# A twelve-stage decoder on one core: the l1 attention in two phases, the l3 convolution as matrix products, and a lower planned cost for products with narrow weights

## The reference, cut to what matters

```python
# l1 attention, 16 heads of 8 features (W block-diagonal per head)
Q, K, V = xh @ Wq, xh @ Wk, xh @ Wv          # xh: layer norm of x, by head
scores  = where(causal, Q @ K.T / sqrt(8), -1e9)
out     = softmax(scores) @ V                # 512 x 512 scores per head
y       = scrambled(out) @ W_O
# l3 attention, a selective scan over 256 channels with 16 states
x, gate = split(layernorm(h) @ in_proj_w + in_proj_b)
x = silu(depthwise_causal_conv(x, conv_w, K=4) + conv_b)
dt_r, Bm, Cm = split(x @ x_proj_w); dt = softplus(dt_r @ dt_proj_w + dt_proj_b)
h_t = exp(dt*A) * h_{t-1} + dt * B_t * x_t;  y_t = h_t . C_t     # 512 steps
out = (sigmoid(gate) * (y + x*D)) @ out_proj_w + out_proj_b + h
```

## Time and profile before

| | |
|---|---|
| median of 3 runs | 2419.95 us (2417.05 to 2420.04) |
| profiled execution, its own time | 2421.95 us |
| its span, first to last instruction | 2420.2 us (1.75 us lie around it) |
| busy: PE, DVE, ACT, POOL | 1886.7, 1694.5, 1019.4, 595.4 us |
| mean granted TensorE clock | 0.833 of full |
| l1 attention, both lanes | about 702 to 1009 us |
| l3 attention, both lanes | about 1711 to 2188 us |

### The profile page before, as it was taken

One profiled execution on the slowest core, in us unless ns is written; L12 is line 12 of the kernel. 1 busy time (PEld: TensorE's weight loads), 2 busy tenths in 40 slices (PEclk: granted clock), 3 DMA queues, 4 the chain that ended last, 5 costly groups with the idle time before them and its releaser, 6 DMA issues. The chain is left out here.

```text
span 2420.2 us, 30708 instructions
## 1 busy us (share of the span) xinstructions
PE 1886.7 (78%) x11122; PEld 1067.2 (44%) x11122; DVE 1694.5 (70%) x3758; ACT 1019.4 (42%) x1610; POOL 595.4 (25%) x528
## 2 busy tenths in 40 slices
PE   4878888889786676799998777669866666689983
PEld 2544645555452222466676655545531222234331
DVE  6666757575767767643637988994479989976556
ACT  1227556565644353443333233232245345335562
POOL 0003323242430010000001643530135534631100
PEclk8888998989996686899999877866668977879975
DMA  4002112120310000000000000000000000000000
GB/s 163 1 0 59 44 47 54 35 67 24 78 62 30 1 1 1 14 10 1 1 1 1 1 1 1 1 1 1 1 0 1 1 0 0 1 1 1 1 5 14
DMA packets 19222, 43.78 MB, mean 18 GB/s; under 512 B 5323, under 2 KB 7935, under 8 KB 18175
## 3 DMA queue, kind: packets, MB, share of 16 engines
q1 hardware_dynamic: 19071, 41.81, 6.1%
HBM read 16.63 MB, written 1.05 MB: 7 GB/s over the span
## 5 line engine op out<-in xcount | busy, mean ns | idle before, releaser
L2275 PE MATMUL lane_banks<-l_attn_lane_hc,base 128*128 128x512 f32 x256 | 168.9, 784 | 91.8 <-DVE l_attn_lane_hc L2430 91.5
L2357 POOL TENSOR_TENSOR l_attn_lane_u<-l_attn_lane_xp,l_attn_lane_bn 128x512 f32<-128x512 f32 x128 | 177.7, 1410 | 208.5 <-ACT l_attn_lane_bn L2328 166.4
L2421 DVE TENSOR_TENSOR_SCAN l_attn_lane_h<-l_attn_lane_da,l_attn_lane_u 128x512 f32<-128x512 f32 x128 | 194.5, 1542 | 6.6 <-ACT l_attn_lane_da L2336 5.5
L595 POOL TENSOR_SCALAR lane_next_rstd<-lane_next_mv 128x4 f32<-128x4 f32 x48 | 12.8, 267 | 717.0 <-DVE lane_next_mv L572 717.0
L1654 ACT ACTIVATE l_ffn_lane_hT<-lane_banks,weights 128x512 f32<-128x512 f32 x128 | 87.9, 687 | 146.2 <-PE lane_banks L1608 145.7
L1451 ACT ACTIVATE l_attn_lane_ex<-lane_banks 128x256 f32<-128x256 f32 (+3 forms) x128 | 82.9, 705 | 149.9 <-PE lane_banks L1409 149.9
L1700 DVE SCALAR_TENSOR_TENSOR l_ffn_lane_eo<-lane_banks,l_ffn_lane_sel,l_ffn_lane_eo 128x128 f32<-128x128 f32 x224 | 63.0, 343 | 96.6 <-PE lane_banks L1630 96.2
L1630 PEld LDWEIGHTS lane_banks<-weights,l_ffn_lane_hT 128*128 128x128 f32 x1024 | 121.2, 194 | 18.6 <-issue 15.2
L2275 PEld LDWEIGHTS lane_banks<-l_attn_lane_hc,base 128*128 128x128 f32 x256 | 52.4, 229 | 170.6 <-DVE l_attn_lane_hc L2430 143.8
L1630 PE MATMUL lane_banks<-weights,l_ffn_lane_hT 128*128 128x128 f32 x1024 | 124.0, 278 | 4.1 <-DVE l_ffn_lane_eo L1700 3.2
L2328 ACT ACTIVATE l_attn_lane_bn<-lane_banks 128x512 f32<-128x512 f32 x64 | 37.9, 594 | 179.1 <-PE lane_banks L2269 179.1
(11 more groups left out here) (526 smaller groups left out, 4693.6 us busy)
## 6 DMA issues: line engine op xcount, KB each, us to landing
f_attn_lane_vb<-f_attn_lane_work SPq DMA_DIRECT2D x192, 64.0 KB, 2.0
weights<-packed SPq DMA_DIRECT2D x1, 4564.5 KB, 13.6
f_attn_lane_work<-f_attn_lane_work SPq DMA_DIRECT2D x64, 64.0 KB, 2.0
f_attn_lane_vb<-f_attn_lane_va SPq DMA_DIRECT2D x8, 512.0 KB, 4.5
f_attn_lane_vb<-f_attn_lane_va SPq DMA_DIRECT2D x8, 384.0 KB, 5.8
weights<-packed SPq DMA_DIRECT2D x1, 2320.0 KB, 8.1
weights<-packed SPq DMA_DIRECT2D x1, 2091.0 KB, 13.9
out<-x SPq DMA_DIRECT2D x4, 256.0 KB, 2.2
```

The lines of the kernel that those rows point to most:

```text
L2275: pe.matmul(ps(2 + c), w("ident"), hc[:, c, :], start=(n == 1), stop=(n == NS)).then_inc(*s.up("state_added"))
L2357: g.tensor_tensor(u[:, i % 3, :], dtx[:, c, :], bn[:, n % 2, :], ALU.mult).then_inc(*s.up("u_ready"))
L2421: v.tensor_tensor_scan(h[:, c, :], da[:, i % 3, :], u[:, i % 3, :], 0.0, ALU.mult, ALU.add).then_inc(*s.up("scanned"))
```

## The change

In the l1 attention the row maxima of all four sets are taken first: the scores come in pairs of banks, two banks being filled while VectorE reduces the other two (32 reductions of two banks in a row of the batch instead of 16 of four). All maxima are negated at once (`mp` has four sets now), turned set by set into the four banks, and added. Then all exps follow: a set has ten steps of one full bank of 512 columns (key tile 0 of one head; tiles 1 and 3 of one head; tile 2 of two heads), which take banks 0 to 2 in turn; `heads` takes a turn too. `ex` has eight slots of 512 columns. `apply` comes three times a set and is placed some steps later, in the next set for the last two. `oS` is double and lies in `rest`. In the l3 attention the taps become eight f32 products with diagonal weights per row of the batch, accumulated in banks 3 and 0; bias and sigmoid read PSUM. `z` has a buffer of its own. The weights of this stage grow from 1510 to 2526 columns. The planner's cost of a product whose weights have at most 32 columns is multiplied by 0.3.

```diff
+def diagonals(w):
+    out = np.zeros((P, A3_C, A3_K, P), w.dtype)
+    for c in range(A3_C):
+        for k in range(A3_K):
+            out[np.arange(P), c, k, np.arange(P)] = w[c * P:(c + 1) * P, k]
+    return out.reshape(P, -1)
...
 def l1_attn(net, ln, row, s, sb, enter):
...
-    mp = sb("mp", [P, NT, R, 32], BF16)
-    ex = sb("ex", [P, 2, R, T])
-    oS = sb("oS", [P, T])
+    mp = sb("mp", [P, SETS, NT, R, 32], BF16)
+    STEPS, SLOTS = 10, 8
+    ex = sb("ex", [P, SLOTS, T])
+    oS = rest
...
+    users = []
+    for j in range(SETS):
+        users += [(j, i) for i in range(4)] + ([("heads", j - 1)] if j else []) + [(j, i) for i in range(4, STEPS)]
+    users.append(("heads", SETS - 1))
+    def turn(user):
+        return ps(users.index(user) % 3)
+    def wait_turn(pe, user):
+        n = users.index(user) - 3
+        if n < 0:
+            pe.wait_ge(*s.at("maxima_ready", n + 4))
+        else:
+            j, i = users[n]
+            if j == "heads":
+                pe.wait_ge(*s.at("cat_ready", i + 1))
+            else:
+                pe.wait_ge(*s.at("exp_done", STEPS * j + i + 1))
...
+        def apply(j, k):
+            yield
+            pe.wait_ge(*s.at("later_only", 8 * j + (2, 6, 8)[k]))
+            if k == 0:
+                if j >= 1:
+                    pe.wait_ge(*s.at("oS_ready", j))
+                else:
+                    pe.wait_ge(*s.at("maxima_ready", SETS))
+                for r in range(R):
+                    last = product(j, r, 0, ex[:, slot(j, r), :])
+            elif k == 1:
+                for r in range(R):
+                    product(j, r, 1, ex[:, slot(j, 4 + r), 0:3 * P])
+                for r in range(R):
+                    last = product(j, r, 3, ex[:, slot(j, 4 + r), 3 * P:T])
...
+        def keyed(j, i):
+            yield
+            wait_turn(pe, (j, i))
...
+            for r, kt in [(i, 0)] if i < 4 else [(i - 4, 1), (i - 4, 3)] if i < 8 else [(i - 8, 2), (i - 6, 2)]:
+                e, p, n = r % 2, 2 * j + r // 2, T - P * kt
+                last = pe.matmul(turn((j, i))[:, at:at + n], ops[half[e], p, 1, tile(kt)], ops[half[e], p, 0, P * kt:T], start=True, stop=True)
+                at += n
+            last.then_inc(*s.up("keyed_in_psum"))
...
+        for n in range(2 * NT * SETS):
+            j, g, b = n // (2 * NT), n // 2 % NT, n % 2
+            t, to = ORDER[g], P * (ORDER[g] + 1)
+            yield
+            if n >= 2:
+                pe.wait_ge(*s.at("row_max", n - 1))
+            for bank in (2 * b, 2 * b + 1):
+                r = late.index(bank)
+                early, p = group[bank ^ 1], 2 * j + r // 2
+                pe.matmul(ps(bank, 0, to), ops[early, p, 0, tile(t)], ops[early, p, 1, 0:to], start=True, stop=False)
+            for bank in (2 * b, 2 * b + 1):
+                last = pe.matmul(ps(bank, to - P, to), net.w16("ident16"), net.w16("later16"), start=False, stop=True)
+            last.then_inc(*s.up("scores_in_psum"))
...
+        for j in range(SETS):
+            for i in range(STEPS):
+                if j >= 1 and i == 0:
+                    yield from apply(j - 1, 1)
+                if j >= 1 and i == 2:
+                    yield from apply(j - 1, 2)
+                if j >= 1 and i == 4:
+                    yield from heads(j - 1)
+                if i == 6:
+                    yield from apply(j, 0)
+                yield from keyed(j, i)
...
+                act.activation(ex[:, slot(j, i), :], turn((j, i)), ACT.Exp, scale=scale).then_inc(*s.up("exp_done"))
...
+            v.tensor_reduce(mx[:, j, t, 2 * b:2 * b + 2], banks(2 * b, 2)[:, :, 0:to], AX.X, ALU.max).then_inc(*s.up("row_max"))
...
 def l3_attn(net, ln, row, s, sb, enter):
...
+        for c in range(C):
+            yield
+            pe.wait_ge(*s.at("xp_ready", c + 1))
+            pe.wait_ge(*s.at("sigmoids_ready", c + 1))
+            for j in range(A3_K):
+                k = A3_K * c + j
+                last = pe.matmul(ps(conv_bank[c]), w("a3_cw", k * P, (k + 1) * P), xp[:, c, j:j + T], start=(j == 0), stop=(j == A3_K - 1))
+            last.then_inc(*s.up("conv_in_psum"))
...
-            act.wait_ge(*s.at("conv_ready", c + 1))
-            act.activation(sgc[:, c, :], cv[:, c, :], ACT.Sigmoid).then_inc(*s.up("conv_sigmoid"))
+            act.wait_ge(*s.at("conv_in_psum", c + 1))
+            act.activation(sgc[:, c, :], ps(conv_bank[c]), ACT.Sigmoid, bias=w("a3_cb", c, c + 1)).then_inc(*s.up("conv_sigmoid"))
...
-        for j in range(A3_K):
-            for c in range(C):
-                k = A3_K * c
-                yield
-                if j == 0:
...
-                    v.tensor_scalar(cv[:, c, :], xp[:, c, 0:T], w("a3_cw", k, k + 1), w("a3_cb", c, c + 1), ALU.mult, ALU.add)\
...
-                    v.scalar_tensor_tensor(out=cv[:, c, :], in0=xp[:, c, j:j + T], scalar=w("a3_cw", k + j, k + j + 1),
-                                           in1=cv[:, c, :], op0=ALU.mult, op1=ALU.add)\
...
-            v.tensor_tensor(xs[:, c, :], cv[:, c, :], sgc[:, c, :], ALU.mult).then_inc(*s.up("xs_ready"))
+            v.scalar_tensor_tensor(out=xs[:, c, :], in0=ps(conv_bank[c]), scalar=w("a3_cb", c, c + 1), in1=sgc[:, c, :],
+                                   op0=ALU.add, op1=ALU.mult).then_inc(*s.up("xs_ready"))
...
     def matmul(self, out, lhsT, rhs, start, stop):
         rows = lhsT.shape[0]
         share = 0.3 if rows <= 32 else 0.6 if rows <= 64 else 1.0
+        share *= 0.3 if lhsT.shape[-1] <= 32 else 1.0
```

More of the change, by code:

```diff
@@ L1402, in tensor @@
-            for g in range(PAIRS):
-                kt, p = g // 2, 2 * j + g % 2
-                n = T - P * kt
-                yield
-                if g >= 1:
-                    pe.wait_ge(*s.at("exp_done", PAIRS * j + g))
-                for e in range(2):
-                    last = pe.matmul(ps(e, 0, n), ops[half[e], p, 1, tile(kt)], ops[half[e], p, 0, P * kt:T], start=True, stop=True)
-                last.then_inc(*s.up("keyed_in_psum"))
-                if g % 2 == 0 and kt >= 1:
-                    yield from apply(j, kt - 1)
@@ L1413, in tensor @@
-            yield from apply(j, NT - 1)
+        for j in range(SETS):
[9 more added lines that the diff above has]
+                yield from keyed(j, i)
+        yield from apply(SETS - 1, 1)
@@ L1414, in tensor @@
+        yield from apply(SETS - 1, 2)
+        yield from norm.tensor(pe, ps(2), norm.to_come)
         yield from heads(SETS - 1)
-        yield from norm.tensor(pe, ps(1), norm.to_come)
         yield
@@ L1465, in gpsimd @@
         g.wait_ge(*s.at("va_zeroed", 2))
-        g.memset(mp[:, :, :, :], 0.0).then_inc(*s.up("va_filled"))
+        g.memset(mp[:, :, :, :, :], 0.0).then_inc(*s.up("va_filled"))
         for i, name in enumerate("qk"):
@@ L1493, in finish @@
             v.wait_ge(*s.at("heads_in_psum", j + 1))
-            heads = ps(2).rearrange("p (t r f) -> p t r f", t=NT, r=R)
+            heads = turn(("heads", j)).rearrange("p (t r f) -> p t r f", t=NT, r=R)
             st.link(v.reciprocal(rden[:, j, :, :], heads[:, :, :, A1_HD]))
@@ L1523, in vector @@
             pair = ops[:, 2 * j:2 * j + 2, 0, :]
-            v.tensor_tensor(pair, pair, bc(ps(0).bitcast(BF16)[:, 0:T], 2), ALU.add).then_inc(*s.up("maxima_ready"))
-            for g in range(PAIRS):
-                kt, h = g // 2, 2 * (g % 2)
-                yield
-                v.wait_ge(*s.at("exp_done", PAIRS * j + g + 1))
-                first = ex[:, kt % 2, h:h + 2, 0:P]
-                v.tensor_tensor(first, first, bc(w("laterT"), 2), ALU.min).then_inc(*s.up("later_only"))
+            v.tensor_tensor(pair, pair, bc(maxima(j), 2), ALU.add).then_inc(*s.up("maxima_ready"))
+        for j in range(SETS):
+            if j == 2:
+                yield from norm.vector(v)
+            for i in (1, 3, 4, 5, 6, 7, 8, 9):
+                if j >= 1 and i == 4:
+                    yield from finish(j - 1)
+                yield from keep_later(j, i)
         yield from finish(SETS - 1)
```

122 lines of the change are left out of this document (53 added, 69 removed).

## The result

The changed kernel takes **2351.6 us**, median of 4 runs (2348.2 to 2353.0), beside 2420.0 for the kernel before on the same chip: ratio 0.9717 [0.9700, 0.9733]. The profiled execution took 2353.02 us (span 2351.2), 68.9 less than the one of before; the forecast was 43.

A forecast was written before the change was run, and what follows sets the result against it. No engine bounds the whole; l1 attention alternates one-engine phases with changeovers, and VectorE bounds l3 attention. -34 and -9 sum to -43 from 2421.95, giving 2379, or a 2377 us median; range 2338 to 2412.

The forecast's parts named there:

- Maxima and exps: l1 attention: per pair of sets 12.3 maxima, 1.4 additions, 12.6 exps; with one changeover 107.7 against 124.7 us a pass.
- rival 1: l1 attention: lanes cover each other, VectorE alone bounds at 92 us a pass; -64 for both, kernel 2347; chance 0.18.
- The extra reduction: l1 maxima: each of eight added reductions costs 0.07 to 0.15 us, 0.9 us for eight; TensorE's filling stays hidden.
- The unpaired products: l1 exps: keyed products in one partition half lose overlap; 2.0 us charged, making TensorE 12.2 us a pair.
- rival 2: l1 exps: TensorE bounds, keyed products never overlap, clock stays near 0.73; no l1 gain, kernel 2411; chance 0.16.
- The clock in the exps: l1 exps: with 50 us of exps at a stretch, TensorE's low clock level expected at the beginning only.
- The first pass: l1 attention: both passes priced alike at -17, -34 together; start and end, 23 to 28 us a pass, stay.
- The plan: Lower planned cost of narrow products changes the order of pieces in three stages; counted 0, ends -10 and +10.
- Stages outside both: Outside l1 and l3 attention: moves of more than 10 us there would show the forecast wrong.
- The l3 attention: Taps off VectorE -19.5, plus 6 for six blocks and 4 for row 0; net -9 us, ends -20 and +29.
- The scans of the other lane cover: l3 attention: the convolution's new wait for the gate's sigmoids and table load is hidden by the other lane's scans.
- The last two rivals: Low-clock TensorE slows l1 exps, 2436, chance 0.06; piece order undoes the gain, within 5 us of 2420, chance 0.04.

The follow-up runs named there:

- by_set: Changed kernel, but each l1 attention set goes through maxima and exps before the next begins; 2388.7 us, 0.9876 of the kernel before.
- conv_split: Changed kernel with each of the four diagonal products of a chunk a piece that others can be planned between; 2344.3 us, 0.9676 of the kernel before.
- conv_free: Changed kernel with the convolution in banks 1 and 2, not waiting for the gate's sigmoids, and the x projection waiting for both chunks; 2329.5 us, 0.9620.
- x_both: Changed kernel with one wait moved: the x projection of chunk 0 waits for both chunks, convolution still in banks 3 and 0; 2333.1 us, 0.9621.
- null_cost: Changed kernel with one planned cost moved for no reason, an activation's fixed part 0.19 instead of 0.18 us; 2359.1 us, 0.9733 of the kernel before.
- l3_only: Kernel before with only the l3 attention's convolution moved to TensorE; 2419.9 us, 0.9994 of the kernel before.

## Why the prediction was right, and where it was not

**Maxima and exps: right.** In the second pass of after the reductions start from 853.3 to 908.0 and the exps from 904.6 to 953.7. To the first exp it is 51.3 us, where the forecast had 49.2 for maxima, 5.6 for additions and 2.5 for the changeover; the exps take 49.8, forecast 50.4. Together 101.1 against 107.7. In the first pass it is 102.4. The 5 to 7 us by which each pass undercuts the forecast are rival 1 in small: lane 0 adds and begins its exps while lane 1 still reduces, 3.4 us by the stamps, and the changeover is gone. The 92 us of that rival were not reached.

**The extra reduction: right**, 0.07 us: by the profile's page 128 of them take 96.2 us, and in before 64 took 91.6. Its cover by TensorE held; VectorE waited 2.9 us.

**The unpaired products: too dear.** 2.0 us a pair of sets were charged, 16 in all at nearly full clock; `by_set` shows 4.2 in all at a clock like that of before, and TensorE had 92.2 / 8 = 11.5 us a pair where 12.2 were forecast. The Trainium skill, "TensorE: Matmul & The Clock Gate", section on packing small matmuls, says that weights load beside a running matmul only when the row groups differ. The prediction concluded that rival 2 would come nearer; `by_set` shows 10% more on the keyed products and not the double. Of the 97.6 us that ScalarE waited in after, 87.6 are the two maxima phases (41.93 and 45.7).

**The clock in the exps: right.** 0.83 and 0.89 in windows that begin with the last maxima, 0.92 from the first exp to the last, "low at the beginning only".

**The first pass: the step that was mis-sized.** The sets were priced at 124.7 us from the second pass for both. In the first pass of before they took 130.6 (first reduction at 724.6, last exp ending near 855.2), and of after 102.4, a gain of 28 and not 17. The prediction's own window of the first pass showed it: 158.3 less 124.7 leaves 34 us for start and end, and it wrote "23 to 28". Start and end, "stay as they are", moved by +6.1 in the first pass and -3.2 in the second. So 34 became 48.9: 11.9 more because both passes' sets came out under 107.7, 5.9 because the first pass had been longer, less 2.9 at the ends.

**The plan: the step that failed.** "The lower cost changes the order of pieces in three stages ... so 0, ends -10 and +10." It is worth 12 to 14 us beside the other two parts, 11.3 of them in the l1 attention, and costs 4 alone. Without it the l1 attention gains 37.6 us, close to the 34 forecast: most of what the sum missed in this stage is this term (the 14.9 us split above by sets and ends are the same 14.9, split by the cost). The forecast took a reordering for noise where the code it was to order had just been rewritten: `apply` comes three times a set with ten keyed pieces around it, and its estimate had been almost three times too high. That this misplaced it is argued, not traced.

**Stages outside both: wrong by its own test** ("moved by more than 10 us"). The l1 cross attention and feed-forward gave 17.8 us, 11.2 with the clock at their beginning and 6.6 because lane 0 came out of the l1 attention that much further ahead; l2 attention and the end gave back 10.6, the stage before the l3 attention gave 7.6. The sum came out 25 us too high, and 11 of them are the plan's in the l1 attention; the clock in untouched stages was no term of it.

**The l3 attention: right in its stage, with luck in the whole.** -9.6 against -9 (its terms add up to -9.5). The diagonal products ran at the full level, 0.592 us each, the cheap end of the 28 to 55 us. One us for each of six blocks is what `conv_split` gave back, 6.4. But row 0, charged with 4, gained 11.0 in the stage before with the old cost and lost 9.2 with the new one, and behind it the clock took 16.6 us with the old cost and gave 4.2 with the new. The plan counts here too: beside the new cost the convolution gives 16.6 us in its stage, beside the old one 9.5. "The scans of the other lane cover" the sigmoids: nearly, 2.3 us in `conv_free` beside `x_both`.

**The last two rivals**: neither showed. TensorE in the exps needed 92.2 / 16 = 5.8 us a set, far from 9.3 (9.0 with the changeover, which that bound leaves out). Rival 2 was priced too low for its own condition: if the keyed products never overlap, TensorE has 19.4 us a pair and not 17, which makes 2431 and not 2411. No run came near either.

## What to carry to other kernels

Merge the phases of several sets when each phase fills another engine: three of four changeovers go, and TensorE's low level falls where it costs nothing. After a rewrite, set the planner's costs again for the new code, and look at every stage that has such pieces: the factor that gained 11 us in the l1 attention came with a longer l2 attention (3.5 us, and 7.5 in the old kernel). Compare any change stage by stage, over several executions: stages that nobody touched moved by up to 18 us with TensorE's clock and the lanes' shift, enough to hide a gain of 10 or to be taken for one. Where two lanes share an engine in a fixed order, look for the piece that waits at its head with the other lane's work behind it; one wait moved later was worth 18 us, more than the convolution's move itself.

## What was not expected of the hardware

TensorE stays at its low level while it is busy. In `null_cost` it is modelled busy 10.00 of 10 us at 2271 with a granted clock of 0.50, and most products of that stage have weights of 32 or 77 rows. The Trainium skill, "TensorE: Matmul & The Clock Gate", Part 1, has the low level as the default and activity as what releases it. Here neither the profile's busy time nor the instructions tell when: the same stage began at the full level and held it for over 100 us with like products. Before and `l3_only` run the same instructions in the same order there, 1.2 us apart and with the same holes up to there; one falls to the low level 102 us in and stays there for some 30 us, the other falls 136 us in. The 1.2 us, what lies ahead of the stage, or something that the profile does not show may decide it; no run separates them.
